# Rope by two VectorE products and a DMA swap, y on ScalarE, bn_aggr, and a loop written out

## What is computed

```
x = x + 0.5 * ffn(layernorm(x))        # norm1
x = x + attn(layernorm(x))             # norm_attn
x = x + 0.5 * ffn(layernorm(x))        # norm2
ffn(x)  = layernorm(x, gamma, beta) @ ternary(weight).T + bias
attn(x): q = x@Wq+bq (16 heads of 128), k, v = x@Wk+bk, x@Wv+bv (4 heads)
         q, k = rope(q), rope(k);  re = xe*cos - xo*sin;  ro = xe*sin + xo*cos
         weights = softmax(q k / sqrt(128)) with j <= i and i - j <= 64
         out = (weights v) @ Wo + bo
```

## Time and profile before

| | |
|---|---|
| median of 3 runs | 892.06 us (890.0 to 892.25) |
| profiled execution | 891.26 us |
| its span, first to last instruction | 889.2 us |
| PE busy | 803.2 us (90%) |
| DVE busy | 692.6 us (78%) |
| ACT busy | 675.0 us (76%) |
| POOL busy | 650.2 us (73%) |
| mean granted TensorE clock | 0.969 |

### The profile page before, as it was taken

The page is one execution under the profiler, slowest core; times in us unless marked ns, Lnnn a source line. Parts: engine busy times, 40 slices in busy tenths (PEclk is TensorE's granted clock), DMA queues, the critical chain, the costliest instruction groups (busy, mean ns, idle before and its releaser), DMA issues.

```text
span 889.2 us, 17647 instructions
## 1 busy us (share of the span) xinstructions
PE 803.2 (90%) x5638; PEld 742.3 (83%) x5638; DVE 692.6 (78%) x1366; ACT 675.0 (76%) x1819; POOL 650.2 (73%) x587
## 2 busy tenths in 40 slices
PE   3689899988998899988999889999899889999994
PEld 2479789988988889887999879998798878999983
DVE  6768966999579885898859986599956988587555
ACT  2489688876887778886878768887688777888861
POOL 2378967887678967788668886788767886778922
PEclk8699999999999999999999999999999999999997
DMA  8031002020020100101020100202002020010100
GB/s 272 24 84 37 1 1 60 2 61 1 1 62 12 48 0 22 40 12 48 0 61 1 35 25 0 62 0 60 0 0 62 0 60 0 9 29 13 49 1 24
DMA packets 26834, 28.36 MB, mean 32 GB/s; under 512 B 1920, under 2 KB 24960, under 8 KB 26752
## 3 DMA queue, kind: packets, MB, share of 16 engines
q1 hardware_dynamic: 26752, 27.55, 10.9%
HBM read 10.76 MB, written 4.19 MB: 17 GB/s over the span
## 4 chain that ended last, share of the span: by engine, by line
PE 54%; DVE 16%; issue 12%; ACT 6%; DVEq 0%; POOL 0%; ACTq 0%
PE job_p L548 18%; PE attn_p L548 14%; PE heads_p L548 8%; PE scores_p L565 7%; DVE y L825 3%; PE probsT_p L605 3%; DVE headsT L704 3%; PE job_p L653 2%; ACT headsT L909 2%; ACT probs L887 2%; DVE rope_cos L745 2%; PE job_p L661 2%; DVE lnT L725 2%; DVE parts L796 1%; DVE probsT L710 1%
## 5 line engine op out<-in xcount | busy, mean ns | idle before, releaser
L984 POOL TENSOR_TENSOR rope_sin<-rope_sin,rope_t 128x512 f32<-128x512 f32 x160 | 211.8, 1324 | 58.4 <-ACT rope_sin L936 58.0
L887 ACT ACTIVATE probs<-scores_p,neg_max 128x128 f32<-128x128 f32 x512 | 181.2, 369 | 55.0 <-DVE neg_max L692 53.9
L548 PE MATMUL attn_p<-wo_s,headsT 128*128 128x256 f32 x1536 | 210.4, 286 | 10.1 <-DVE headsT L704 10.1
L548 PE MATMUL job_p<-xnT,wq_s 128*128 128x512 f32 x768 | 210.1, 409 | 0.6 <-DVE v_s L750 0.6
L548 PEld LDWEIGHTS attn_p<-wo_s,headsT 128*128 128x128 f32 x1536 | 194.6, 191 | 17.4 <-DVE headsT L704 14.3
L974 POOL TENSOR_TENSOR probs<-probs,inv_sum 128x512 f32<-128x512 f32 x128 | 137.3, 1073 | 77.1 <-DVE inv_sum L698 77.0
L995 POOL TENSOR_TENSOR q_s<-rope_cos,rope_sin 128x512 f32<-128x512 f32 x124 | 161.2, 1300 | 27.1 <-POOL rope_sin L984 10.9
L548 PEld LDWEIGHTS job_p<-xnT,wq_s 128*128 128x128 f32 x768 | 139.0, 193 | 26.7 <-DVE v_s L750 1.5
L935 ACT ACTIVATE rope_sin<-job_p,columns_s 64x512 f32<-64x512 f32 x160 | 109.8, 686 | 60.2 <-PE job_p L548 58.2
L745 DVE SCALAR_TENSOR_TENSOR rope_cos<-job_p,columns_s,rope_t 128x512 f32<-128x512 f32 x160 | 118.4, 743 | 44.5 <-ACT rope_sin L936 33.4
L704 DVE SCALAR_TENSOR_TENSOR headsT<-heads_p,columns_s,headsT 128x512 fp32r<-128x512 f32 x128 | 95.0, 742 | 59.3 <-ACT headsT L909 59.3
(11 more groups left out here) (78 smaller groups left out, 1136.9 us busy)
## 6 DMA issues: line engine op xcount, KB each, us to landing
v_odd<-v_s SPq DMA_DIRECT2D x64, 192.0 KB, 3.6
x_in<-x SPq DMA_DIRECT2D x16, 256.0 KB, 3.9
out<-x_res SPq DMA_DIRECT2D x16, 256.0 KB, 2.2
staging_q<-wo SPq DMA_DIRECT2D x2, 512.0 KB, 10.6
staging_q<-wq SPq DMA_DIRECT2D x2, 512.0 KB, 10.7
x_res<-wo SPq DMA_DIRECT2D x2, 512.0 KB, 3.5
rope_cos<-wk SPq DMA_DIRECT2D x1, 512.0 KB, 6.7
rope_sin<-wq SPq DMA_DIRECT2D x1, 512.0 KB, 7.8
```

What stands on the lines that cost most here:

```text
L548: mm = nc.tensor.matmul(dst, a(p), b(q), start=first and clears and i == 0, stop=last and i == 2, skip_group_check=True)
L887: ins = nc.scalar.activation(probs[:, i, k, :], scores_p[i][:, k, :], ACT.Exp, bias=neg_max[:, i, k:k + 1], accum_out=row_sum[:, i, k:k + 1])
L984: nc.gpsimd.tensor_tensor(rope_sin[:, r, :], rope_sin[:, r, :], sin_t, ALU.mult).then_inc(rope_sined, 1)
```

## The change

1. Rope: VectorE makes both products from the bank, (bank + bias) * sin first, then (bank + bias) * cos, and that second one frees the bank. SyncE then issues two DMAs of 64 partitions by 512 elements (128 KB each) that copy the halves of rope_sin crosswise into a new buffer rope_swap; GpSimd adds rope_cos and rope_swap, in the prologue too. There are four buffers of each (ROPES). The sign in the sin table moves with the order of product and swap. ScalarE has no part in the rope any more.
2. y is written by ScalarE, as x * rstd + shift, with shift = -mean * rstd made on GpSimd in two more small instructions a half.
3. Mean and variance come from bn_aggr, two instructions a half in place of six.
4. The hardware loop is written out: the six middle passes are instructions of their own, with constant waits.
5. VECTOR, SCALAR, GPSIMD and SYNC have new orders. TENSOR has the order of before.

```diff
-        rope_cos = sb("rope_cos", [P, 2, SEQ])
-        rope_sin = sb("rope_sin", [P, 2, SEQ])
+        rope_cos = sb("rope_cos", [P, ROPES, SEQ])
+        rope_sin = sb("rope_sin", [P, ROPES, SEQ])
+        rope_swap = sb("rope_swap", [P, ROPES, SEQ])
...
-            with eng.Fori(1, BATCHES - 1) as b:
+            for b in range(1, BATCHES - 1):
                 yield Phase("middle", b)
...
+            def swap_halves(phase, x):                     # SyncE
+                n = ROPED.before(phase, x)
+                r = n % ROPES
+                sp.wait_ge(rope_sined, n + 1)
+                if n >= ROPES:
+                    sp.wait_ge(rope_added, n + 1 - ROPES)
+                for to, at in ((slice(0, HALF), slice(HALF, P)), (slice(HALF, P), slice(0, HALF))):
+                    sp.dma_start(rope_swap[to, r, :], rope_sin[at, r, :]).then_inc(rope_swapped[r], 16)
...
                 if kind in ("Q", "K"):                     # VectorE, take
-                    dve.wait_ge(rope_swapped, ROPED.after(phase, x))
...
+                    if n >= ROPES:
+                        dve.wait_ge(rope_swapped[r], 32 * (n // ROPES))
+                    nc.vector.scalar_tensor_tensor(
+                        out=rope_sin[:, r, :], in0=bank[:, :], scalar=bias, in1=sin_t,
+                        op0=ALU.add, op1=ALU.mult).then_inc(rope_sined, 1)
+                    if n >= ROPES:
+                        dve.wait_ge(rope_added, n + 1 - ROPES)
                     nc.vector.scalar_tensor_tensor(
                         out=rope_cos[:, r, :], in0=bank[:, :], scalar=bias, in1=cos_t,
                         op0=ALU.add, op1=ALU.mult).then_inc(rope_cosed, 1)
...
+                    ins = nc.vector.bn_aggr(stats[:, 2 * m + k, :], parts[:, 2 * m + k, :])
...
+            def normalize(phase, x):                       # now on ScalarE
+                act.wait_ge(rstd_ready, 2 * NORMED.after(phase, norm))
+                    act.wait_ge(job_ready, y_read_before(phase, x))
+                    ins = nc.scalar.activation(y[:, k, :], src[:, at, :], ACT.Identity, bias=shift[:, at:at + 1],
+                                               scale=rstd[:, at:at + 1])
...
+                nc.gpsimd.tensor_tensor(minus_mean[:, half], stats[:, half, 0], minus_one[:, half],
+                                        ALU.mult).then_inc(rstd_step, 1)
+                nc.gpsimd.tensor_scalar(tmp[:, half], stats[:, half, 1], factor, added, ALU.mult,
+                                        ALU.add).then_inc(rstd_step, 1)
...
-                nc.gpsimd.tensor_tensor(rope_sin[:, r, :], rope_sin[:, r, :], sin_t, ALU.mult).then_inc(rope_sined, 1)
...
+                pool.wait_ge(rope_swapped[r], 32 * (n // ROPES + 1))
+                pool.wait_ge(rope_cosed, n + 1)
```

More of the change, by code:

```diff
@@ L49 @@
 BLOCKS = SEQ // P
+ROPES = 4
 EC = E // P
@@ L95 @@
 VECTOR = """
[L96 to L112, removed]
+    heads13p probsT14p K1c Q4c max0c evac0p stats0p heads14p probsT15p inv0c max1c
@@ new lines @@
+    Q5c w8f inv1c heads15p V10c Q6c probsT0c max2c Q7c evac1p inv2c
+    stats1p YT0p heads0c probsT1c K2c max3c Q8c end_YT0p heads1c probsT2c inv3c
+    Q9c max4c stats0n tern0i tern1i inv4c stats1n heads2c V11c probsT3c max5c
+    FO0p YT1p inv5c heads3c Q10c end_YT1p probsT4c Q11c w9f max6c inv6c
+    FO1p heads4c probsT5c K3c max7c YT0n inv7c heads5c end_YT0n Q12c probsT6c
+    max8c w0i FO0n astats0n YT1n heads6c Q13c probsT7c end_YT1n inv8c Q14c
+    max9c heads7c w1i FO1n inv9c astats1n probsT8c max10c Q15c inv10c heads8c
@@ L113 @@
+    probsT9c w2i w3i w4i XT0n max11c XT1n inv11c heads9c probsT10c w5i
+    w6i w7i K0n max12c Q0n inv12c heads10c probsT11c max13c Q1n inv13c
+    V00n heads11c probsT12c max14c Q2n inv14c heads12c probsT13c Q3n max15c inv15c
+    V01n
 """
 SCALAR = """
[L115 to L130, removed]
@@ L131 @@
-    exp15c mask1n
+    probsT14p w8f exp0c heads14p probsT15p mask2c norm0p exp1c mask3c heads15p V10c
+    probsT0c exp2c mask4c heads0c probsT1c YT0p norm1p exp3c heads1c probsT2c mask5c
+    w9f exp4c heads2c mask6c V11c probsT3c exp5c norm0n heads3c YT1p mask7c
+    probsT4c exp6c heads4c probsT5c mask8c norm1n exp7c heads5c w0i YT0n probsT6c
+    mask9c exp8c heads6c probsT7c mask10c w1i YT1n w2i anorm0n heads7c exp9c
+    probsT8c mask11c exp10c anorm1n heads8c probsT9c w3i w4i XT0n mask12c XT1n
@@ L132 @@
+    w5i w6i w7i exp11c heads9c probsT10c mask13c exp12c mask14c heads10c probsT11c
+    exp13c V00n mask15c heads11c probsT12c exp14c mask0n heads12c probsT13c exp15c V01n
+    mask1n heads13c
 """
 GPSIMD = """
[L134 to L144, removed]
@@ L228, in after, with turn @@
         return self.before(phase, item) + self.weight(item)
-    def parity(self, phase, item):
-        assert self.in_pass("middle") % 2 == 0
-        return self.before(Phase(phase.name, 1), item) % 2
+    def turn(self, phase, item, buffers):
+        return self.before(phase, item) % buffers
 def of(*kinds):
@@ L374, in block_kernel @@
         job_ready = sem("job_ready")
-        rope_swapped = sem("rope_swapped")
+        rope_swapped = [sem(f"rope_swapped{i}") for i in range(ROPES)]
         rope_cosed = sem("rope_cosed")
@@ L461, in norm_of, with variance_terms, y_read_before @@
             return (("norm2", *x[1:]), x_res) if x[2] == "prev" else (("norm1", *x[1:]), x_in)
-        def variance_factor(norm):
-            return 1.0 if norm[0] == "norm_attn" else 1.0 + LN_EPS
+        def variance_terms(norm):
+            return (1.0, LN_EPS) if norm[0] == "norm_attn" else (1.0 + LN_EPS, LN_EPS * LN_EPS)
+        def y_read_before(phase, x):
+            own = ("XT" if x[0] == "anorm" else "YT", *x[1:])
+            held = [z for z in Y_HALVES.items if z[2] in phase.parts and z[0] in ("YT", "XT")]
+            at = held.index(own)
+            return BANKED.after(phase, held[at - 1]) if at else BANKED.start(phase)
         def v_part(i, s):
@@ L916, in probsT_high @@
                                      ACT.Copy).then_inc(probsT_hi, 1)
+            def normalize(phase, x):
+                (norm, src), m = norm_of(x), x[1]
+                act.wait_ge(rstd_ready, 2 * NORMED.after(phase, norm))
+                if phase.name == "prologue" and x == ("norm", 0, "next"):
+                    act.wait_ge(scale_ready, 1)
+                else:
+                    act.wait_ge(job_ready, y_read_before(phase, x))
+                for k in range(2):
+                    at = 2 * m + k
+                    ins = nc.scalar.activation(y[:, k, :], src[:, at, :], ACT.Identity, bias=shift[:, at:at + 1],
+                                               scale=rstd[:, at:at + 1])
+                ins.then_inc(y_ready, 1)
             def take(phase, x):
```

127 lines of the change are left out of this document (39 added, 88 removed).

## The result

The changed kernel takes **871.41 us** (median of 4 runs, 870.55 to 872.35) against 892.15 (890.0 to 892.63, 4 runs) for the kernel before on the same chip: a ratio of 0.9777, 95% interval 0.9757 to 0.9797. It is faster, by 20.7 us. Forecast were 44. The profiled execution's span is 869.6 us (889.2 before).

What follows compares the result with a forecast made beforehand. TensorE's line, busy 98.8 of 105.79 us, sets the pass. From 891.26 us: -7.7 (loop), six times (-4.9 - 1.8 - 0.6 + 1.5) = -34.8, -2.8 (first pass), +1.5 (prologue) gave 847.5, predicted 848; range 834 to 888.

Steps and rivals of the forecast that it cites:

- part 4: Swap by DMA: +1.5 us a pass for T0 and what follows from a late y, bounds 0 to about 3.
- My -2.8: First pass: a shorter wait for lnT takes 2.8 us off.
- rival C: Swap waits on GpSimd's line, before probs0, probs3, probs6 and probs8, make it slower than before: 910 us, chance 0.13.
- Part 1: Loop written out: 1.55 us for each of five returns, -7.7 us, with 0 taken for fetching instructions.
- Part 2: VectorE's new work: load -0.7 us a pass; TensorE's waits closed by -4.9, -1.8 and -0.6 us a pass.
- The -4.9 for lnT: TensorE before FO0n: 3.2 us of waiting, 0.2 of start-up and 1.5 of slow running go in each pass.
- The two smaller terms: TensorE's waits before YT1p for V11's bank, -1.8 us a pass, and before XT1n for Q15's bank, -0.6.
- Part 3: ScalarE and GpSimd lose rope work and gain y work, both ending near 60 of 98 us; nothing booked.
- Part 5: Outside the middle passes: first pass 2.8 us off, prologue +1.5 (0 to 4), end 0 within 1.
- A: VectorE, strictly in order, takes TensorE's place; half of the 7.3 us a pass stays open: 870 us, chance 0.17.
- B: lnT waits behind GpSimd's residual0 addition, 1.7 us late, and slow running comes back: 863 us, chance 0.13.
- D: The written-out program doesn't run like a held loop, all gains eaten: 889 to 894 us, chance 0.05.

Runs made afterwards that it cites:

- k1_behind_probs0: The changed kernel with K1's addition moved behind scale0p and probs0 in GpSimd's list: 847.04 us, ratio 0.9487.
- y_on_act: The kernel before with the loop written out, y on ScalarE and bn_aggr, rope as before: 861.2 us, ratio 0.9639.
- loop_out: The kernel before with only the loop written out: 882.7 us, ratio 0.9881.
- k1_and_probs_first: k1_behind_probs0 with probs8 and probs9 also ahead of the additions of Q13 and Q14 in GpSimd's list: 841.47 us, ratio 0.9434.
- y_dve_both_late: The changed kernel with y back on VectorE, and in GpSimd's list K1 behind probs0, bias0 and bias1 two steps later: 861.68 us, ratio 0.9661.
- loads_late: The changed kernel with SyncE issuing the two loads of x after the swaps of K1, Q4 and Q5: 853.73 us, ratio 0.957.

## Why the prediction was wrong

**The step that failed is part 4's price for the pass's start.** It was booked as "+1.5 us a pass for T0 and what follows from a late y", bounds 0 to about 3. The place and the mechanism were right: K1 first in GpSimd's line, its swap behind six other issues, probs0 behind both. The size was wrong three times over.

- *In the pass.* The walk had scale0p start near 9 us and probs0 end near 12. Measured from K1's start, in the pass shown: the addition at 10.3, scale0p at 11.5, probs0's end at 14.1. I took 0.6 for an issue and 3.0 for a landing; there one of the copies took 1.45 to issue, and K1's own two swaps landed in about 4.1 (the six in 3.5, median) beside two loads of 4.8. T0 is then up to 1.8 late, and V10's bank, which the sum named only as "what follows", 1.2. Undoing it gives 3.2 us a pass (100.9 to 97.7), where 1.5 was booked.
- *In the first pass.* I priced the late start only where old work covers it. The first pass has none: 5.2 us of waiting at T0, and 5.4 us come back in k1_behind_probs0. My -2.8 for this pass left it out. The -2.8 itself isn't seen either: in y_on_act the wait for lnT of this pass is gone (2.53 us in loop_out) and the pass takes 95.8 us in both; why, stays open.
- *In the middle, once more.* T8 waits 1.07 in each pass behind Q13's swap, one of rival C's four places. I had seen a margin under 1 us in each of them and booked nothing. This one was cheap, 0.4 a pass, 1.2 in the first pass and 1.4 at the end.

With K1 alone moved, the kernel stands at 847.04, where 848 was forecast. That it is so near is luck, since the 848 still holds the 9 us booked for this wait and 1.5 for the prologue: against the forecast the prologue is then 2.5 us and the six passes 4.6 us shorter, the first pass 2.2 and the end 3.4 longer.

**Part 1, the loop.** -7.7 forecast, 8.2 measured in the middle passes. Right.

**Part 2, VectorE.** The -4.9 for lnT: 3.17 us of waiting went to 0.53 in y_on_act, and the pass by 3.6 in the mean (104.2 to 100.6), with that last 0.53 still open. In the kernel after no FO0n has a bracket. The slow running went with the wait: between 519 and 523 us, behind it, the kernel before had a granted clock of 0.71; the kernel after has 1.00 behind its FO0n (508 to 512), and 1.00 in the middle passes where it was 0.98. The two smaller terms came too: the wait before YT1p is 0.3 us a pass in the mean, as forecast, and the one before XT1n is gone. lnT's row there answers to the earlier trace rows:

```profile
506.15 0.68 DVE L711 TENSOR_TENSOR lnT<-ln_full,lnT 128x512 fp32r<-128x512 f32 x1
...
506.16 1.82 POOL L963 TENSOR_TENSOR x_in<-x_in,rows_s 128x512 f32<-128x512 f32 x1
```

All of part 2 and the loop, without part 4's term, gave 105.8 - 1.55 - 7.3 = 96.95 a pass. Five of six passes are 97.0 to 97.4 in k1_and_probs_first, so this sum held.

The fourth middle pass is 1.3 to 3.1 us longer than its neighbours in all seven versions with the swap and y on ScalarE. In each of them one transfer is slow there: the second swap of Q7 lands in 3.7 to 4.2 us, where it takes 2.3 in the third and the fifth pass. GpSimd's addition for Q7 stands behind it, in k1_behind_probs0 in the third and in the fourth pass:

```profile
357.31 1.29 POOL L955 TENSOR_TENSOR q_s<-rope_cos,rope_swap 128x512 f32<-128x512 f32 x1 [0.24 <-DMA rope_swap<-rope_sin]
...
456.30 1.29 POOL L955 TENSOR_TENSOR q_s<-rope_cos,rope_swap 128x512 f32<-128x512 f32 x1 [1.67 <-DMA rope_swap<-rope_sin]
```

Behind it y waits on ScalarE for 3.44 us and not 1.81, and TensorE 0.90 for heads. In y_dve_both_late that swap is slow too (3.5), but the pass is no longer than the others. What slows this one swap is not tested. In all eight traces a transfer of instructions (16 KB, queue q8 of the DMA view; 45 in the kernel after, 17 in the one before) runs beside Q7's two swaps in the fourth pass and none of that queue in the third and the fifth; that it holds the swap up is likely, and would be a small price of the written-out program.

**Part 3.** y on ScalarE takes 1.09 us a pair and not 0.84. ScalarE (502 us, about 520 forecast) and GpSimd (462, about 480) came out slightly lighter. VectorE's load in a pass fell by 6.8 us and not by 0.7: the four small instructions that I left out count, lnT is no longer stretched, and bn_aggr is cheap, 0.25 for a pair where 0.4 was taken:

```profile
456.09 0.25 DVE L788 BATCH_NORM_AGGREGATE stats<-parts 128x2 f32<-128x6 f32 x2
```

**Part 5.** The prologue was 0.7 shorter, not 1.5 longer: two waits for the cos product, 0.63 and 0.66 before, went. But over the runs here the first pass starts between 45.9 and 49.1, so this is not to be told from nothing. The end was called 0 and is +4.4. The experiments show what of it is orders: 1.0 by K1, 1.4 by probs8 and probs9, 1.4 by ScalarE's heads and masks. 0.65 is left over and not explained; the chain of y in the epilogue is there, with lnT waits of 3.84 and 2.63 where before it had 3.33 and 2.63.

**The rivals.** A (VectorE takes over) did not happen: even with y back on it (y_dve_both_late) a pass is only 2.3 us longer than in k1_behind_probs0. Its figure, 870, is met by accident. B (lnT behind GpSimd) did not happen at FO0n: the 2.4 us addition now ends before lnT starts. The rows above show the two engines side by side there, and this time lnT took its 0.68 and GpSimd's addition 1.82, where 1.29 is usual. By the rule of the Trainium skill ("SBUF — State Buffer", "Who interferes with whom") the two exclude each other; the trace agrees that somebody pays, 0.53 us here, and it need not be VectorE. C (the swap on GpSimd's line) is what happened, at two of its four places. It was worked out only as a catastrophe, with landings beyond 5.4 us; it came with landings of 2.2 to 4.5 us in the six swaps at a pass's start, by order and queue, and cost 24 us and not 60. D is refuted by loop_out; at most the longer fourth pass is of its kind.

## What to carry to other kernels

A step that waits for a transfer, put first in an in-order engine's list, delays everything behind it by issue, queue and landing together. Put it behind the step that the critical engine needs next, and count the issues already in the DMA queue ahead of it. Price such a stall in each kind of pass: where older work covers it, it costs a little, and in the first pass all of it. And when a busy instruction is moved to another engine, look for who waits for its *reading* to end: moving y back made an addition on GpSimd wait 8 us, which no view of VectorE's load would show.

## What was not expected of the hardware

- A swap of 128 KB from SBUF to SBUF lands in 2.2 to 2.3 us when no other transfer is near (483 us in the kernel after; 2.3 is also the median of all 320). At a pass's start it is 3.5 (2.2 to 4.5) behind four copies of v and two loads of 256 KB, and 2.9 (2.2 to 3.1) in loads_late, where only the copies are ahead. SyncE's issue of a swap takes 0.46 to 0.60 us there, and up to 1.5 elsewhere.
- GpSimd can pay for VectorE as VectorE does for GpSimd: the 128x512 addition takes 1.30 us in the median, and 1.82 beside a 0.68 us subtraction of VectorE.
- ScalarE takes 0.60 us for a 256-wide y from SBUF, hardly less than the 0.63 for a 512-wide lnT. The two are not the same instruction (y has a scale and a bias per partition, lnT is a copy), so these rows don't say what width alone costs.
